# Router gathers released by TensorE's place in the experts' products instead of a full stop every sixteen

## What is computed

```python
xn = _layernorm(x)
x = x + _L0_gnn_ref(xn, edge_index, ...) + _L0_mix_ref(xn[None], ...)[0]
x = x + _L0_ffn_ref(_layernorm(x)[None], ..., L0_ffn_edge_index)[0]

# in _L0_ffn_ref, M nodes, 4 heads, 4 experts
h = (x_flat @ W_gat).reshape(M, HEADS, NUM_EXPERTS)
e = leaky_relu(a_src[src] + a_dst[dst], 0.2)
alpha = exp(e - segment_max(e, dst)[dst]) / (segment_sum(...)[dst] + 1e-16)
agg = segment_sum(h[src] * alpha[:, :, None], dst) + b_gat
scores = _layernorm(agg).reshape(M, HEADS, NUM_EXPERTS).mean(1)
# the two best experts of each node, weighted by a softmax of their scores
out = sum over experts of g_e * (gelu(x @ W1[e] + b1[e]) @ W2[e] + b2[e])
```

## Time and profile before

| | us |
|---|---|
| three runs, median | 4269.84 |
| three runs, lowest and highest | 4265.19, 4272.2 |
| span of the profiled execution | 5331.2 |
| of it, graph stage, POOL's gathers (130 to 2641) | 2511 |
| scatters to the next block (2641 to 2833) | 192 |
| experts and router (2833 to 4967) | 2134 |
| tail (4967 to 5331) | 364 |

### The profile page before, as it was taken

One profiled execution on the slowest core, in us unless ns is written; L12 is line 12 of the kernel. 1 busy time (PEld: TensorE's weight loads), 2 busy tenths in 40 slices (PEclk: granted clock), 3 DMA queues, 4 the chain that ended last, 5 costly groups with the idle time before them and its releaser, 6 DMA issues. The chain is left out here.

```text
span 5331.2 us, 46344 instructions
## 1 busy us (share of the span) xinstructions
PE 3564.3 (67%) x12937; PEld 2313.0 (43%) x12938; DVE 2082.9 (39%) x4892; ACT 801.1 (15%) x1970; POOL 2832.6 (53%) x2937
## 2 busy tenths in 40 slices
PE   0688888888757777777626377768685777789200
PEld 0455555555445455555413154444453454455100
DVE  5456655665546555544311020211111120212378
ACT  5111211111101111111101011111111111112000
POOL 2666666666666666666655623653636444630420
PEclk9889899998878888888767588888787788899655
DMA  7444444444445555555512111211112111211387
GB/s 250 128 109 115 112 111 112 112 115 112 112 111 148 138 153 154 162 152 152 125 33 61 18 49 28 58 38 48 35 50 43 44 48 36 60 50 48 118 254 253
DMA packets 381413, 540.57 MB, mean 101 GB/s; under 512 B 120314, under 2 KB 297818, under 8 KB 381143
## 3 DMA queue, kind: packets, MB, share of 16 engines
q0 software_dynamic: 119136, 234.44, 20.0%
q1 hardware_dynamic: 243119, 288.12, 16.8%
q10 hardware_dynamic: 19016, 16.48, 0.9%
HBM read 392.03 MB, written 146.74 MB: 101 GB/s over the span
## 5 line engine op out<-in xcount | busy, mean ns | idle before, releaser
L788 POOL DMA_INDIRECT rows<-xn_rows,gsrc x1664 | 1606.6, 965 | 908.5 <-issue 459.8
L1357 POOL DMA_INDIRECT nb<-route_rows,idx x1024 | 1000.3, 977 | 897.7 <-DVE msg L1432 480.9
L1093 PE MATMUL PS<-rows,oh 128*128 128x257 f32 x3328 | 910.0, 427 | 351.9 <-issue 220.0
L1686 PE MATMUL PS<-arena,hid 128*125 128x256 f32 x3200 | 865.1, 422 | 408.5 <-issue 298.6
L1686 PEld LDWEIGHTS PS<-arena,hid 128*125 128x125 f32 x3200 | 662.9, 209 | 621.3 <-issue 502.6
L1093 PEld LDWEIGHTS PS<-rows,oh 128*128 128x128 f32 x3328 | 693.8, 214 | 488.8 <-issue 296.6
L1621 DVE TENSOR_TENSOR y_sb<-PS,b_b 125x512 f32<-125x512 f32 x200 | 128.7, 685 | 1781.4 <-remote 975.2
L1678 PE MATMUL PS<-x2g,arena 128*128 128x500 f32 x1600 | 722.6, 610 | 147.3 <-issue 94.0
L1678 PEld LDWEIGHTS PS<-x2g,arena 128*128 128x128 f32 x1600 | 313.5, 197 | 541.6 <-issue 473.0
L1647 ACT ACTIVATE hid<-PS,b_sb 128x500 f32<-128x500 f32 x400 | 269.9, 677 | 1109.9 <-PE PS L1678 688.9
L1165 PE MATMUL PS<-own_w,p_t 128*125 128x512 f32 x400 | 231.2, 662 | 77.7 <-ACT s_t L1053 54.5
(11 more groups left out here) (304 smaller groups left out, 3086.8 us busy)
## 6 DMA issues: line engine op xcount, KB each, us to landing
y_rows<-y_sb SPq DMA_DIRECT2D x100, 512.0 KB
arena<-y_rows SPq DMA_DIRECT2D x100, 512.0 KB
rows<-xn_rows,gsrc POOLq DMA_INDIRECT x1664
nb<-route_rows,idx POOLq DMA_INDIRECT x1024
sum_rows<-kept SPq DMA_DIRECT2D x104, 128.5 KB
x_rows<-x SPq DMA_DIRECT2D x100, 128.0 KB
hid<-x_rows SPq DMA_DIRECT2D x100, 128.0 KB
m_in<-sum_rows SPq DMA_DIRECT2D x100, 125.5 KB
```

What stands on the lines that cost most here:

```text
L788: pool.indirect_dma_start(out=rows[w][h][:, q, 0:D], out_offset=None, in_=xn_rows, in_offset=bass.IndirectOffsetOnAxis(ap=gsrc[:, s * HU + ...
L1093: last = mm(SUM[:, 0:D + 1], oh[w][h][:, q, :], rows[w][h][:, q, :], start=h == 0 and q == 0, stop=h == 1 and q == HU - 1)
L1357: pool.indirect_dma_start(out=nb[b % NBUF][:, c, :], out_offset=None, in_=route_rows, in_offset=bass.IndirectOffsetOnAxis(ap=idx[:, b * W ...
L1686: last = mm(Y[j % 2][e // 2][0:NP, (e % 2) * D:(e % 2 + 1) * D], hid[:, 4 * e + k, j * NP:(j + 1) * NP], w2_sb[:, e, k, :], start=k == 0, ...
```

## The change

The constant REST goes, and with it the stop at every sixteenth gather. Each gather now waits for the gather four before in all cases. A new function gives for gather n a place in PE's work: n of 1024 gathers at 5.65 tiles a batch, 64 to a batch. In the first half of a group's four tiles the place is a step of the first product (`s_hp`), in the second half a finished tile (`s_y`). A gather waits for that place wherever it differs from that of the gather before. `unit_after` is the same as before, with the number 5.65 under a name.

```diff
-REST = 16
+TILES_A_BATCH = 5.65
...
 def unit_after(b):
 
-    t = int((b + 1) * 5.65) + 3
+    t = int((b + 1) * TILES_A_BATCH) + 3
     return t if t % 4 < 2 else t + 4 - t % 4
+
+
+def reached(n):
+
+    tiles = max(n, 0) * TILES_A_BATCH / W
+    g, f = int(tiles // 4), tiles % 4 / 4
+    half = f >= 0.5
+    return g, half, g * 4 + int((f - 0.5) * 8) if half else g * 16 + int(f * 32)
...
                     for c in range(W):
-                        if (b or c) and c % REST == 0:
-                            for q in range(AHEAD):
-                                pool.wait_ge(s_nb[q], (b * W + c) // AHEAD * 16)
-                        elif b or c >= AHEAD:
+                        _, half, value = reached(b * W + c)
+                        if value and reached(b * W + c - 1) != reached(b * W + c):
+                            pool.wait_ge(s_y if half else s_hp, value)
+                        if b or c >= AHEAD:
                             pool.wait_ge(s_nb[c % AHEAD], (b * W + c) // AHEAD * 16)
```

## The result

The changed kernel takes 4147.16 us (median of four runs, 4144.19 to 4151.77), beside 4268.53 of the kernel before: a ratio of 0.971, 95% interval 0.9696 to 0.9725, some 121 us less. Forecast was 4188, with a range of 4125 to 4310. So the sign held, and the gain is half as large again as the 82 us forecast.

A forecast was written before the change was run, and what follows sets the result against it. POOL's router gathers were taken to bound the experts at 1497 us; without the stops PE's 1415 us would bound them, so 82 us come off 4270, giving 4188 us, range 4125 to 4310.

The forecast's parts named there:

- the 82 us forecast: Experts stage: time the change takes off the path, 1497 us before less 1415 after.
- The sum before: Experts before the change, POOL as bound: 1433 us of router gathers plus 64 us behind the last one, 1497 us.
- PE's own floor: Experts' products on PE alone: first group 67 us, 23 groups at 55.6, last 68.9, together 1415 us.
- POOL's end after: Experts after the change: POOL's gathers end at 1319 us, and 64 us more make 1383 us.
- PE becomes the bound: Experts after the change: POOL's 1383 us lies below PE's 1415, with 32 us to spare.
- The 62 us: Whole kernel: the account of the recorded trace without pauses gave 4208 us, 62 us (1.5%) under the measured median.
- The extra wait: Added wait on 455 POOL gathers: price taken near 0 if already met, at most 0.41 us each.
- (a): Rival: experts' gathers are already hidden and PE is the bound before as after, 4270 us; chance 0.18.
- (b): Rival: the added wait between gathers holds POOL, up to 0.41 us 455 times, 4280 to 4343 us; chance 0.22.
- (c): Rival: PE really pauses beside bursts of gathers, even spacing removes another 62 us, 4126 us; chance 0.08.
- (d): Rival: all DVE work of a batch holds POOL, 195 us, POOL bound on both sides, 4156 us; chance 0.04.
- The test I had named for the gates: POOL gaps at gathers with a new, open wait: 0.30 us means right, 0.5 us or more wrong.

The follow-up runs named there:

- the second trace: The kernel before, unchanged, profiled once more to check its long recorded trace: 4277.51 us, span 4275.7 us.
- the 4096 met waits: Kernel before without stops or gates, plus four waits ahead of each gather for a semaphore that long has its value: 4155.34 us, ratio 0.9721.
- the first trace: The kernel before, unchanged, as profiled for the prediction: span 5331.2 us, where its three runs had a median of 4269.84 us.
- its repetition: The changed kernel run once more, unaltered, side by side with the version without stops and gates: 4148.37 us, ratio 0.9707.
- the version with late gates: The changed kernel without the gates of the first batch, the other fifteen batches keeping theirs: 4151.56 us, ratio 0.9713.

## Why the prediction came out as it did

**The sum before** was 1497 us for the experts; the second trace has 1553.9 (2388.6 to 3942.5), 57 more. The gathers take 1474.1 of it instead of 1433. The plain price (967 us of gathers, 312 of gaps) was right. The 63 stops cost 134 us instead of 124: I took the gap from one row, 2.27, where the mean is 2.43. Gathers beside DVE's work lose 49 us in sum (1015.8 in place of 967), where I had counted 13 gathers at 2.4 us, 31. The one gather a batch was right, but there are 15 of them, 2.6 us more each (40 us), and smaller losses make up the rest. Late landings apart from the stops, which I had left out, add 13.

The rest of the 57, 16 us, is the tail, where a step was wrong. The rows are of the second trace: DVE meets the last batch, PE takes the lanes' ends, and then the last group begins.

```profile
3864.25 0.17 DVE L1403 COPY m_run<-m_run 128x4 f32<-128x4 f32 x1 [36.33 <-DMA nb<-route_rows,idx]
...
3879.44 1.03 PE L1692 MATMUL PS<-wide,ends 128*20 128x128 f32 x4 [39.04 <-DVE ends L1450]
3882.28 28.86 PE L1678 MATMUL PS<-x2g,arena 128*128 128x500 f32 x64 [1.81 <-DVE endt L1466]
```

I let PE be three steps into the last group and wait for ACT's Exp. It stands at the transposes of the lane ends instead, which wait for the records of the last batch too; only then its 16 steps begin, all of them. From the end of the last gather to the last product it is 79.8 us, and not 64. On PE's own side I had counted those transposes, with the 68.9 us of its last group; on POOL's I had left them out.

**PE's own floor**, 1415 us, looks exact, but part of that is luck. Without stops and gates, the last product ends 1414.0 us after the first gather starts, 23 groups take 55.5 to 55.6 us each and the last 69.9. DVE and PE still wait there for the last gathers:

```profile
3722.86 0.17 DVE L1400 COPY m_run<-m_run 128x4 f32<-128x4 f32 x1 [4.30 <-DMA nb<-route_rows,idx]
...
3738.10 1.03 PE L1689 MATMUL PS<-wide,ends 128*20 128x128 f32 x4 [7.06 <-DVE ends L1447]
3740.94 28.55 PE L1675 MATMUL PS<-x2g,arena 128*128 128x500 f32 x64 [1.81 <-DVE endt L1463]
```

In the first trace of the kernel before, from which I took the 68.9 us, the last gathers had landed long ago, and the same wait of PE's was 2.99 us:

```profile
4900.36 0.61 PE L1692 MATMUL PS<-wide,ends 128*20 128x128 f32 x4 [2.99 <-DVE ends L1450]
4903.20 30.12 PE L1678 MATMUL PS<-x2g,arena 128*128 128x500 f32 x64 [2.23 <-DVE endt L1466]
```

So some 4 us of the 1414.0 are still POOL's (7.06 - 2.99), and PE's own floor is near 1410, an estimate. The 68.9 held some 3 us of that trace's slower products (30.12 against 28.55 in the first of them, 22.46 against 20.99 in the last), and these filled the place.

**POOL's end after** failed by the same terms. I had 1383 us, 32 under PE's floor. It is 1426.2: 1346.4 us of gathers instead of 1319 (14 us more beside DVE, 11 of late landings, 2 of the gates at the start), and 79.8 instead of 64 behind them. So the step "PE becomes the bound" failed: **POOL stays last, by 11 us** over the 1415, and the last group takes 81.2 us. Even without gates POOL is still the later one by some 4 us: there the last product ends 79.6 us behind the last gather, as in the change.

**The gain.** 1553.9 - 1426.2 = 127.7 us in the traces, 121 to 126 in the runs, against 82. My sum before was 57 us too short and the one after 11, because there PE's floor hid most of the same terms; the difference, 46, is what the forecast missed. The 62 us by which the account of the recorded trace fell short of the median were the sign of it. Against the second trace (4275.7 us) it is 68 us: these 57 and 42 of the graph stage's gathers (2119 us from the first to the last instead of 2077), less 31 for a tail of 333 us instead of 364. I had read the shortfall as an error to live with, though it was three quarters of the gain I forecast.

**The extra wait.** Its price, held near 0, is 0 for a wait that is met, as the 4096 met waits show. What I didn't ask is what the added wait does to the wait beside it. It pushes the landing's wait off the gather, and that costs some 0.5 us wherever a landing is late. The upper row I had for it, 0.71 us behind a stop's last wait, was this effect: at a stop the last landing's wait also stands by itself, and with one wait alone most stops lost 0.5 us. The reason that I had named ("that gather had to be decoded after the wait") may hold, but it is still an argument, since the order alone is shown; the condition I had wrong.

The Trainium skill, Perfetto Trace Analysis, Identifying Dependency Chains, says that an instruction with waits on several engines may have EventSemaphore instructions put ahead of it; the 458 of them are these. By its section DMA Instruction — SWDGE (GPSIMD) a gather's own wait is held in a queue while the sequencer goes on. The gaps agree with that: 0.30 us with a met wait, and 0.46 for a late one that rides.

**The rivals.** (a), gathers already hidden, falls with the version without gates: DVE waits 173.6 us for gathers in the second trace of before, and 4.3 in that version. (b), the added wait holds POOL, falls: the gates cost 10 us, where 114 (455 x 0.25) would have been needed. (c), 4126 us, was nearer in time than the forecast, but not for its reason: PE runs at 55.6 us a group without any gate, so there was no pause for an even spacing to remove. (d), all of DVE's two-input work holds POOL, came nearest of all (4156) and falls as well: the loss beside DVE is 49 us before and 45 after, not 195. I had also written that the rows bear the rule out for the scans. They do so for one gather alone: in the earlier trace rows the gather at 3436.77 runs beside the scans in 1.00 us, and only the one at 3439.37 takes 3.34. The rule behind it, from the Trainium skill, GPSIMD Engine Reference, Specifications, names a contention; the 195 us that I made of it are about four times what the gathers lost here.

**Where it would show.** The gaps of 2.27 us are gone, and gathers that lag stand at 1.25 us. The wait for DVE's buffers is near zero as I had said, but that was no sign: the second trace of before has none either. The test I had named for the gates, 0.30 or 0.5 us at a gather with a new wait, had both answers: 0.30 where the landing was in time, 0.98 where it was late.

## What to carry to other kernels

A wait for everything in flight costs the whole way of the last transfer each time. Where a wait for the transfer four before already bounds the queue, take the stop out before pacing anything; here pacing brought nothing, because the engine that was paced was itself the late one. If a transfer must carry two waits, write first the one that is likely to be late. And when an account of the stages misses the measured time by as much as the gain that is forecast, look for the missing piece before the sum is used.

## What the runs showed of the hardware

The position of a wait has a price, a met wait has none: four met waits more on each of 1024 gathers leave the gap at 0.30 us, while a late landing takes 0.46 us on the gather and about 1.0 us ahead of it. The durations of the separate waits don't show it (17 to 43 ns in the change, although landings are late there); the gap of the next gather does.

A gather beside DVE's record scans is either not held at all or held to their end. In the change, the gathers that start early in a batch's 20 scans take 0.94 to 1.00 us. In each batch but the last, one starts later, and it takes 2.55, 3.34 or 3.50 us, as its start has it: it always ends 0.80 us behind the last scan. The rows show DVE's scans, which end at 2677.02, and two of the gathers beside them:

```profile
2671.70 5.32 DVE L1444 TENSOR_TENSOR_SCAN rec<-dd,rec,msg 128x64 f32<-128x64 f32 x20
```

```profile
2674.01 0.94 POOL L1365 DMA_INDIRECT nb<-route_rows,idx  x1 [0.30 <-issue]
2675.26 2.56 POOL L1365 DMA_INDIRECT nb<-route_rows,idx  x1 [0.30 <-issue]
```

All fourteen traces have it so, with 13 to 15 held gathers each, 0.79 to 0.81 us behind the scans. Why the early ones pass isn't shown, nor whether the scans or the copy of Y behind them let the held one go.

One profiled execution of the kernel before took 25% longer than all its runs, with PE's pauses spread through it, and another one agreed with the runs within 0.1%. Without a second trace, such rows can't be told from the kernel's own.

In the change, its repetition, the version with late gates and the one with met waits ahead, gaps above 0.5 us stand at the same gathers, 333, 663, 773 and 883 (counted from 0), all of them multiples of 110 apart. The four kernels share gaps at 603 and 810 too, but those stand five places behind a gather held beside DVE, and the ones at 333, 663, 773 and 883 don't. With the landing's wait first, the change keeps only the one at 333, while the version with met waits has gaps of 1.35 to 2.36 us at 223, 553 and 993, in the same steps of 110. What lies behind that isn't shown.
